# A later wait in the down product and an early Gelu table load in a fused decoder kernel

## Chip, cores and metric

The kernel runs on one core of a Trainium2 chip. The metric is the device time of one execution in microseconds (us), lower is better. The kernel before takes 1753.62 us, the median of three runs (1751.96 to 1753.97).

## What is computed

Eight sequences of 512 rows with 512 features go through one decoder layer, all in f32 unless said otherwise:

```python
x = layernorm(x + retention(x) + conv5(x))             # per-feature decay scan, then a 512x512 product
x = layernorm(x + mlstm_attention(q=x, k=ctx, v=ctx))  # 8 heads, gates from q, k, v
h = gelu([x, stats(x)] @ r1_w.T + r1_b)                # router, 6 statistics per row
probs = softmax(h @ r2_w.T)                            # 32 experts, each row picks two
# each expert takes its 160 best rows (capacity int(1.25 * 4096 / 32))
up = xe @ w_up.T; hact = silu(up[:, :1024]) * up[:, 1024:]
ye = hact @ w_down.T                                   # 512 outputs, weighted, added to the rows
# 16 adapters, one for every two experts: the same form with 128 hidden units
x = layernorm(x + experts + adapters)
```

## The kernel before

The work has three parts, one after the other. Every engine has its own program, and the order of work on each engine is written out by hand; engines wait for each other on counting semaphores.

**The pipeline over the sequences** (`run_pipeline`, L127) runs ten steps, n = 0 to 9. In step n the retention and the first norm of sequence n (flag `a`, true for n up to 7), the attention of sequence n - 1 (flag `s`, n from 1 to 8) and the last norm and router of sequence n - 2 (flag `r`, n from 2 to 9) are interleaved. ScalarE's order is in its `step` (L1054): the gates of sequence n (`gates_0`, `gates_1`, L955 to L969, which end with an Exp and a Ln), the copy of the router's statistics (`router_stats`, L1035), then `gates_3` and `gates_4` (L971 to L981, three Copies; the first waits for VectorE's running maximum, L1340), then the two Gelus of the router (`router_2`, L1042, which wait for TensorE's products L718 and L723), then `gates_5` (a Copy and two Exps, L1002 to L1004) and so on. Exp, Ln and Gelu need different function tables; the compiler puts an ACT_TABLE_LOAD straight before the ACTIVATE that needs another table, behind that instruction's waits written in the kernel. TensorE's router logits (L730) wait for the second Gelu, and its products for the attention state (L642) come after them. VectorE's work on the states (L1263) waits for L642.

**The selection** (L805 to L840 on TensorE) finds the rows of each expert.

**The experts**, 32 of them (`run_experts`, L133: two written out, 28 in a loop that handles two per turn, two written out). TensorE's order for one expert (`expert`, L888) is:

- `up` nine times (L853 to L870): chunk j of the hidden units, 128 of the gate and 128 of the values; j = 8 is the adapter's. Each f32 matmul counts as two in the trace, so this is 16 times 9 = 144 matmuls of 160 columns per expert on line L869. ScalarE makes the Silu of each chunk (L1144), VectorE multiplies (L1748, for the adapter L1750) and writes `hact[:, j]`. The steps of VectorE are named `mul0` to `mul8`.
- `rows_in` (L843 to L851): five transposes of the next expert's gathered rows (not in the last expert).
- `down` (L872 to L886): nine chunks again, 18 matmuls of 512 columns on L881 for the first 128 rows (k = 0), then 72 small ones on L884 for the other 32 rows (k = 1). At its head it waits for the weights, for `mul8`, and for the product before to have been read.

SyncE's queue loads the weights of expert e + 2 as soon as expert e has freed the buffers; GpSimd gathers rows and scatters results with indirect DMAs. Behind the last expert there is a tail: a last scatter, a gather of the rows that it touched, their norm and their store, while the other rows were normalised and stored beside the last two experts.

Of the kernel before, what the change touches and what calls it, by code (L numbers as in the profile page):

```python
# [21 lines left out]
ACT = mybir.ActivationFunctionType  # L22
# [3 lines left out]
NB, T, D = 8, 512, 512  # L26
# [3 lines left out]
TAPS, PAD = 5, 2  # L30
# [5 lines left out]
J = INTER // P  # L36
# [108 lines left out]
def decoder_kernel(nc, xT_d, kT_d, v_d, decay_d, WT_d, b_d, cw_d, cb_d, wi_d, wf_d, ib_d, fb_d, ln_d,  # L145
# [5 lines left out]
    with ctx:  # L151
# [5 lines left out]
        def steps(name, names, lead=3):  # L157
            p = Steps(sem(name), names, lead)
            every[name.split("_")[-1]].append(p)
            return p  # L160
# [36 lines left out]
        room = Room(arena, ROOM)  # L197
        WT = room.take(C, D)
        wgq = room.take(C, 32)
        wgk = room.take(C, 32)  # L200
# [10 lines left out]
        r1s = room.take(RH)  # L211
# [7 lines left out]
        xT = room.take(C, T + 2 * PAD)  # L219
# [14 lines left out]
        wgv = hg[:, 0, 0:C * 32].rearrange("p (c g) -> p c g", c=C)  # L234
        stT = gpart
        zeros = room.take(2 * D)
# [6 lines left out]
        Fr = [room.take(INT, dt=BF16) for _ in range(2)]  # L243
        Ff = g_rel.rearrange("p a t -> p (a t)")
        Fm = room.take(INT, dt=BF16)
        gm = room.take(T)
        bfs = [room.take(T, dt=BF16) for _ in range(2)]
# [22 lines left out]
        zeros = zeros[:, 0:D]  # L270
# [6 lines left out]
        oh0 = room.take(TB, NE)  # L277
        oh1 = room.take(TB, NE)
        wsum = room.take(TB)


        Wb = bank[0:2]
# [150 lines left out]
        up_v = steps("up_vector", [f"mul{j}" for j in range(J + 1)], 2)  # L433
# [106 lines left out]
        def _(pe):  # L540
# [285 lines left out]
            for i in range(2 * NT // LG):  # L826
                pe.wait_ge(*li_v.at(f"oh{i}", b0))
                k, lh = i * LG // NT, Lh[i % 3]
# [43 lines left out]
            def down(e):  # L872
                pe.wait_ge(ld_wd[e.slot], e.landed())
                pe.wait_ge(ld_ad[e.slot], e.landed())
                pe.wait_ge(*up_v.at(f"mul{J}", e))
                for k in range(2):
                    pe.wait_ge(*yr_v.at(f"y{k}", e - 1))
                    for j in range(J + 1):
                        w = wd[e.slot][:, j, :] if j < J else ad[e.slot]
                        if k == 0:  # L880
                            m = pe.matmul(Yb[0][:, :], hact[:, j, 0:P], w, start=(j == 0), stop=(j == J))  # L881
                        else:
                            for c in range(C):
                                m = pe.matmul(Yb[1][CAP2 * c:CAP2 * (c + 1), 0:P], hact[:, j, P:CAP],  # L884
                                              w[:, c * P:(c + 1) * P], start=(j == 0), stop=(j == J))
                    m.then_inc(yr_t(f"y{k}"), 1)  # L886
# [13 lines left out]
        def _(act):  # L900
# [5 lines left out]
            def inputs(b, c):  # L906

                if c == 0:
                    act.wait_ge(ld_x, b.line(16, 16))
                    act.wait_ge(*re_t.at(f"w{TB - 1}", b - 2))  # L910
                act.activation(ST[b.slot][:, c, :], xc[:, c, :], ACT.Identity, scale=a_one[:, c:c + 1])\
                    .then_inc(re_a(f"u{c}"), 1)
                act.activation(cv[b.slot][:, c, :], xc[:, c, :], ACT.Identity, scale=cw[:, c, PAD:PAD + 1],
                               bias=cb[:, c:c + 1]).then_inc(re_a(f"cv{c}"), 1)

            def raw_rows(b, tb):
                if tb == 0:
                    act.wait_ge(*ro_t.at("h1", b - 3))
                act.wait_ge(*re_t.at(f"w{tb}", b))
                act.activation(raw[:, tb, :], Wb[tb % 2][:, :], ACT.Copy).then_inc(n1_a(f"raw{tb}"), 1)  # L920

            def norm1_out(b):
                act.wait_ge(*n1_p.at("shift", b))
                act.wait_ge(*l2_v.at("sum", b - 2))
                for tb in range(TB):
                    act.activation(x1[b.slot][:, tb, :], raw[:, tb, :], ACT.Identity, scale=rs1[:, tb:tb + 1],
                                   bias=nb1[:, tb:tb + 1]).then_inc(n1_a(f"out{tb}"), 1)

            def norm3_out(b):
                act.wait_ge(*l2_p.at("shift3", b))  # L930
                act.wait_ge(*ro_v.at("stats", b - 1))
                for tb in range(TB):
                    act.activation(x2[b.slot][:, tb, :], x2[b.slot][:, tb, :], ACT.Identity, scale=rs3[:, tb:tb + 1],
                                   bias=nb3[:, tb:tb + 1], accum_out=rsum[:, tb:tb + 1]).then_inc(n3_a(f"out{tb}"), 1)

            def squares(b):
                act.wait_ge(*n3_a.at(f"out{TB - 1}", b))
                act.wait_ge(*ro_p.at("l2", b - 1))
                act.wait_ge(*ro_t.at("lg", b - 1))
                act.wait_ge(*ro_v.at("stats", b - 1))  # L940
                act.wait_ge(st_dum, 64)
                for tb in range(TB):
                    m = act.activation(sqr[tb], x2[b.slot][:, tb, :], ACT.Square,
                                       accum_out=rsq[:, tb:tb + 1])
                m.then_inc(n3_a("sq"), 1)
# [60 lines left out]
            def decays(b, h):  # L1006

                act.wait_ge(*bc_t.at(f"bc{h}", b))
                if h >= 4:
                    act.wait_ge(*pv_t.at(f"pv{h // 2 - 2}", b))  # L1010
                else:
                    act.wait_ge(*pv_t.at(f"pv{h // 2 + 2}", b - 1))
                if h == 0:
                    act.wait_ge(*ga_a.at("gcol", b))
                d = Dm[h // 2 % 2][:, h % 2 * T:(h % 2 + 1) * T]
                for tb in range(TB):
                    m = act.activation(d[:, tb * P:(tb + 1) * P], Bb[:, tb * P:(tb + 1) * P], ACT.Exp,  # L1017
                                       bias=gcol[b.slot][:, tb, h:h + 1])
                m.then_inc(at_a(f"exp{h}"), 1)
# [15 lines left out]
            def router_stats(b):  # L1035
                act.wait_ge(*ro_t.at("st", b))
                act.activation(stT[0:NSTAT], Tb[0:NSTAT, :], ACT.Copy).then_inc(ro_a("st"), 1)
# [6 lines left out]
            def router_3(b):  # L1044
# [2 lines left out]
                act.activation(lg, Wb[0][:, 0:TB * NE].rearrange("p (a e) -> p a e", a=TB), ACT.Copy)\  # L1047
                    .then_inc(ro_a("lg"), 1)

            def router_4(b):  # L1050
                act.wait_ge(*ro_v.at("lsub", b))
                act.activation(pr, pr, ACT.Exp).then_inc(ro_a("exp"), 1)

            def step(n, a, s, r, x1, x2):  # L1054

                if s:
                    decays(n - 1, 2)
                if x1:
                    inputs(n + 1, 0)
                if a:  # L1060
                    raw_rows(n, 0)
                if s:
                    decays(n - 1, 3)
                if x1:
                    inputs(n + 1, 1)
                if a:
                    raw_rows(n, 1)
                if x1:
                    inputs(n + 1, 2)
                if a:  # L1070
                    raw_rows(n, 2)
                if x1:
                    inputs(n + 1, 3)
                if s:
                    decays(n - 1, 4)
                if r:
                    norm3_out(n - 2)
                if a:
                    raw_rows(n, 3)
                if s:  # L1080
                    decays(n - 1, 5)
                if r and s:
                    squares(n - 2)
                if a:
                    norm1_out(n)
                    queries(n, (0, 1))
                if s:
                    decays(n - 1, 6)
                if a:
                    queries(n, (2, 3))  # L1090
                if r:
                    router_1(n - 2, a)
                if r and not s:
                    squares(n - 2)
                if s:
                    decays(n - 1, 7)
                if a:
                    gates_0(n)
                    gates_1(n)
                if r:  # L1100
                    router_stats(n - 2)
                if a:
                    gates_3(n)
                    gates_4(n)
                if r:
                    router_2(n - 2, 0)
                    router_2(n - 2, 1)
                if a:
                    gates_5(n)
                    gates_f(n)  # L1110
                    decays(n, 0)
                    gates_g(n)
                if r:
                    router_3(n - 2)
                if a:
                    decays(n, 1)
                    first_state(n)
                if r:
                    router_4(n - 2)
# [50 lines left out]
        def _(dve):  # L1170
            start(dve, "vector")

            for t in (xT[:, :, 0:PAD], xT[:, :, PAD + T:], wgq, wgk, wgv, gm, Fr[0], Fr[1], stT, r1s, bfs[0], bfs[1], zeros):
                dve.memset(t, 0.0)
            for t in va:
                dve.memset(t[:, :, NH * VW:], 0.0)
# [880 lines left out]
```

## Time and profile before

| what | value |
|---|---|
| median of three runs | 1753.62 us |
| profiled execution | 1756.21 us |
| its span, first to last instruction | 1754.4 us |
| TensorE matmul busy | 1504.7 us, 86% |
| VectorE busy | 758.7 us, 43% |
| ScalarE busy | 486.9 us, 28% |
| mean granted TensorE clock | 0.926 |

The profile comes from one execution; it lies 2.59 us above the median and 1.81 us of it lie outside the span. In the tables PE is TensorE's matmul side, PEld its weight loads, DVE VectorE, ACT ScalarE, POOL GpSimd, SP SyncE. A granted clock of 1.0 is 2.4 GHz, 0.5 is 1.2 GHz. The pipeline fills about the first 640 us, the selection runs to about 750 us, the experts to 1735 us.

### The profile page before, as it was taken

The numbers are of one execution on the slowest core, as the hardware profiler recorded it, in microseconds if no ns is written. First come the engines' busy times: TensorE is split into PE (matmuls) and PEld (weight loads), VectorE is DVE, ScalarE is ACT, GpSimd is POOL, SyncE is SP. The second block draws the span as 40 slices with busy tenths as digits, with TensorE's granted clock in tenths as the row PEclk, the third lists the DMA queues.
The fourth block names the chain that finished last, engine by engine and source line by source line (L and its number), as shares of the span: only waits on it lengthen the run. The fifth ranks groups of instructions, "written<-read, shape, count | busy, mean of one in ns | idle before, by whom it ended". The sixth has DMA issues, their size and how long they took to land.

```text
span 1754.4 us, 28619 instructions
## 1 busy us (share of the span) xinstructions
PE 1504.7 (86%) x11038; PEld 1158.6 (66%) x11076; DVE 758.7 (43%) x1783; ACT 486.9 (28%) x1165; POOL 309.4 (18%) x399
## 2 busy tenths in 40 slices
PE   3589999899897540389999999999999999999995
PEld 2256656556555420278787888878788887878884
DVE  7458999999978569811111111111111111111143
ACT  3446666676664220011111110111111011111123
POOL 3101121111111200011121212112121211212125
PEclk9698998998997765589999999999999999999998
DMA  5203123133211054046776767676776767677696
GB/s 156 72 1 115 48 79 104 48 90 95 75 49 49 1 202 169 0 156 214 285 246 259 264 222 282 214 283 240 264 264 226 278 215 278 239 271 257 230 344 209
DMA packets 92191, 311.02 MB, mean 177 GB/s; under 512 B 42455, under 2 KB 46557, under 8 KB 82781
## 3 DMA queue, kind: packets, MB, share of 16 engines
q1 hardware_dynamic: 78876, 287.87, 44.8%
q0 software_dynamic: 13248, 22.29, 5.6%
q8 instruction: 39, 0.64, 0.1%
q14 instruction: 28, 0.22, 0.0%
HBM read 273.18 MB, written 36.96 MB: 177 GB/s over the span
## 4 chain that ended last, share of the span: by engine, by line
PE 71%; DVE 18%; issue 6%; ACT 3%; DMA 1%; POOL 1%; SPq 0%; DVEq 0%; POOLq 0%; ACTq 0%
PE bank L869 36%; PE banks L881 15%; PE bank L582 5%; PE banks L884 4%; DVE arena L1212 3%; DVE arena L1587 2%; PE banks L672 2%; PE bank L718 1%; PE bank L584 1%; DVE arena L1202 1%; PE banks L683 1%; PE banks L656 1%; DVE arena L1378 1%; PE bank L642 1%; DVE arena L1233 1%
## 5 line engine op out<-in xcount | busy, mean ns | idle before, releaser
L869 PE MATMUL bank<-arena 128*128 128x160 f32 x4608 | 636.0, 300 | 0.7 <-issue 0.7
L869 PEld LDWEIGHTS bank<-arena 128*128 128x128 f32 x4608 | 628.3, 191 | 7.3 <-issue 7.3
L1144 ACT ACTIVATE arena<-bank 128x160 f32<-128x160 f32 x288 | 87.4, 303 | 835.2 <-PE bank L869 835.2
L1748 DVE TENSOR_TENSOR arena<-arena,bank 128x160 f32<-128x160 f32 x256 | 82.3, 322 | 459.4 <-ACT arena L1144 408.8
L881 PE MATMUL banks<-arena 128*128 128x512 f32 x576 | 255.6, 598 | 8.9 <-DVE arena L1750 8.9
L1914 POOL DMA_INDIRECT acc_rows<-arena,keep x64 | 102.8, 1606 | 651.9 <-DVE arena L1693 634.1
L881 PEld LDWEIGHTS banks<-arena 128*128 128x128 f32 x576 | 106.9, 190 | 138.6 <-issue 132.5
L1691 DVE TENSOR_SCALAR arena<-banks,keep 128x512 f32<-128x512 f32 x32 | 24.0, 750 | 318.8 <-PE banks L884 316.6
L582 PE MATMUL bank<-arena 128*128 128x512 f32 x256 | 121.7, 620 | 30.8 <-DVE arena L1212 30.8
L582 PEld LDWEIGHTS bank<-arena 128*128 128x128 f32 x256 | 49.8, 200 | 85.1 <-issue 77.1
L1212 DVE SCALAR_TENSOR_TENSOR arena<-arena 128x512 f32<-128x512 f32 x128 | 96.1, 750 | 3.4
L1017 ACT ACTIVATE arena<-bank,arena 128x128 f32<-128x128 f32 x256 | 72.5, 370 | 43.1 <-PE bank L557 43.1
L884 PEld LDWEIGHTS banks<-arena 128*32 128x32 f32 x2304 | 60.9, 110 | 24.3 <-issue 24.3
L672 PE MATMUL banks<-arena 128*128 128x96 f32 x512 | 71.6, 300 | 2.3 <-DVE arena L1293 2.3
L672 PEld LDWEIGHTS banks<-arena 128*128 128x128 f32 x512 | 68.7, 214 | 7.2 <-issue 7.2
L1902 POOL DMA_INDIRECT arena<-x_rows,keep x64 | 64.2, 1003 | 36.4 <-POOL keep L1894 26.6
L884 PE MATMUL banks<-arena 128*32 128x128 f32 x2304 | 69.5, 274 | 0.0
L1894 POOL COPY keep<-keep 128x2 int32 (+1 forms) x64 | 29.3, 458 | 204.9 <-DVE keep L1682 119.3
L718 PE MATMUL bank<-arena 128*128 128x512 f32 x128 | 60.7, 618 | 0.7 <-ACT arena L1031 0.7
L814 PE MATMUL bank<-arena 128*128 128x1 f16 x30 | 5.6, 185 | 59.2 <-DVE arena L1587 59.2
L1130 ACT ACTIVATE arena<-banks 128x512 f32<-128x512 f32 x32 | 19.1, 597 | 118.7 <-PE banks L850 114.9
L718 PEld LDWEIGHTS bank<-arena 128*128 128x128 f32 x128 | 23.9, 197 | 30.9 <-issue 29.5
(252 smaller groups left out, 1632.9 us busy)
## 6 DMA issues: line engine op xcount, KB each, us to landing
arena<-in_wup SPq DMA_DIRECT2D x32, 4096.0 KB, 12.5
arena<-in_wdn SPq DMA_DIRECT2D x32, 2048.0 KB
arena<-in_aup SPq DMA_DIRECT2D x32, 512.0 KB, 11.7
arena<-in_xT SPq DMA_DIRECT2D x8, 1024.0 KB, 5.3
arena<-in_kT SPq DMA_DIRECT2D x8, 1024.0 KB, 7.2
arena<-in_v SPq DMA_DIRECT2D x32, 256.0 KB, 7.8
x_rows<-arena SPq DMA_DIRECT2D x8, 1024.0 KB, 4.4
acc_rows<-arena SPq DMA_DIRECT2D x8, 1024.0 KB, 6.7
```

Of the source, the lines that this page charges most:

```text
L582: pe.matmul(w[:, :], ST[b.slot][:, c, rows], WT[:, c, :], start=(c == 0), stop=False)
L672: pe.matmul(Pp[:, r * T + tb * PVN:r * T + (tb + 1) * PVN], Dm[j % 2][:, r * T + tb * P:r * T + (tb + 1) * P], va[b.slot][:, tb, h * VW:h ...
L718: pe.matmul(Wb[k][:, :], r1x[:, c, k * P:(k + 1) * P], x2T[:, c, :], start=(c == 0), stop=False)
L869: m = pe.matmul(u[:, g * CAP:(g + 1) * CAP], w, xeT[:, c, :], start=(c == 0), stop=(c == C - 1))
L881: m = pe.matmul(Yb[0][:, :], hact[:, j, 0:P], w, start=(j == 0), stop=(j == J))
L884: m = pe.matmul(Yb[1][CAP2 * c:CAP2 * (c + 1), 0:P], hact[:, j, P:CAP], w[:, c * P:(c + 1) * P], start=(j == 0), stop=(j == J))
L1017: m = act.activation(d[:, tb * P:(tb + 1) * P], Bb[:, tb * P:(tb + 1) * P], ACT.Exp, bias=gcol[b.slot][:, tb, h:h + 1])
L1144: act.activation(sg[k], Ub[k][:, 0:CAP], ACT.Silu).then_inc(up_a(f"silu{j}"), 1)
L1212: dve.scalar_tensor_tensor(row, xT[:, c, k:k + T], cw[:, c, k:k + 1], row, ALU.mult, ALU.add).then_inc(re_v(f"tap{i}_{c}"), 1)
L1748: dve.tensor_tensor(hact[:, j, :], sg[k], u, ALU.mult).then_inc(up_v(f"mul{j}"), 1)
L1902: pool.indirect_dma_start(out=xg[e.slot][:, cols], out_offset=None, in_=rows, in_offset=bass.IndirectOffsetOnAxis(ap=idx_g[e.slot][:, k:k ...
L1914: pool.indirect_dma_start(out=rows, out_offset=bass.IndirectOffsetOnAxis(ap=idx_s[e.slot][:, k:k + 1], axis=0), in_=yy[e.slot][:, cols], i ...
```

## The change

```diff
+        tab = room.take(2)[0:1, 0:1]
...
             def down(e):
                 pe.wait_ge(ld_wd[e.slot], e.landed())
                 pe.wait_ge(ld_ad[e.slot], e.landed())
-                pe.wait_ge(*up_v.at(f"mul{J}", e))
+                pe.wait_ge(*up_v.at(f"mul{J - 1}", e))
                 for k in range(2):
                     pe.wait_ge(*yr_v.at(f"y{k}", e - 1))
                     for j in range(J + 1):
+                        if k == 0 and j == J:
+                            pe.wait_ge(*up_v.at(f"mul{J}", e))
                         w = wd[e.slot][:, j, :] if j < J else ad[e.slot]
...
+            def table(f):
+                act.activation(tab, tab, f)
+
...
                 if r:
                     router_stats(n - 2)
+                    table(ACT.Gelu)
                 if a:
                     gates_3(n)
                     gates_4(n)
...
-            for t in (xT[:, :, 0:PAD], xT[:, :, PAD + T:], wgq, wgk, wgv, gm, ...
+            for t in (xT[:, :, 0:PAD], xT[:, :, PAD + T:], wgq, wgk, wgv, tab, gm, ...
                 dve.memset(t, 0.0)
```

TensorE now enters `down` when `mul7` is there and waits for `mul8` only ahead of the ninth chunk of the first 128 rows. ScalarE gets one more ACTIVATE, a Gelu of one element in place, in each of the eight steps with `r`, between the copy of the router's statistics and `gates_3`. VectorE gets one more memset at its start.

## Rows read from the trace of the kernel before

**Rows 1.** The page: the chain that ended last, by line, share of the span

```profile
PE bank L869 36%; PE banks L881 15%; PE bank L582 5%; PE banks L884 4%; DVE arena L1212 3%; DVE arena L1587 2%; PE banks L672 2%; PE bank L718 1%; PE bank L584 1%; DVE arena L1202 1%; PE banks L683 1%; PE banks L656 1%; DVE arena L1378 1%; PE bank L642 1%; DVE arena L1233 1%
```

**Rows 2.** The chain in order of time, first and third expert: start us, us, what

```profile
751.90 21.38 PE bank L869 x144
...
815.05 19.77 PE bank L869 x144
...
835.64 7.99 PE banks L881 x18
...
845.73 19.77 PE bank L869 x144
```

**Rows 3.** Waits of TensorE by line: us in total, times, longest

```profile
PE banks L881 <- DVE arena L1750: 8.9, 32, 1.0
...
PE bank L730 <- ACT arena L1042: 5.9, 6, 1.8
```

**Rows 4.** Timeline, weight loads into down, four kinds of expert: start, length, idle before

```profile
926.46 0.60 PEld L850 LDWEIGHTS banks<-keep,arena 128*128 128x128 f32 x5
927.50 0.30 PEld L881 LDWEIGHTS banks<-arena 128*128 128x128 f32 x2 [0.44 <-DVE arena L1750]
...
958.17 0.30 PEld L881 LDWEIGHTS banks<-arena 128*128 128x128 f32 x2 [0.51 <-issue]
...
1693.54 0.30 PEld L881 LDWEIGHTS banks<-arena 128*128 128x128 f32 x2 [0.61 <-issue]
...
1724.31 0.30 PEld L881 LDWEIGHTS banks<-arena 128*128 128x128 f32 x2 [1.16 <-issue]
```

**Rows 5.** Timeline of TensorE's matmuls in the same expert as the first of rows 4

```profile
926.59 0.71 PE L850 MATMUL banks<-keep,arena 128*128 128x128 f32 x5
```

**Rows 6.** Timeline of VectorE in that expert: mul7, then mul8

```profile
924.95 0.32 DVE L1748 TENSOR_TENSOR arena<-arena,bank 128x160 f32<-128x160 f32 x1 [1.85 <-ACT arena L1144]
927.13 0.32 DVE L1750 SCALAR_TENSOR_TENSOR arena<-arena,bank 128x160 f32<-128x160 f32 x1 [1.85 <-ACT arena L1144]
```

**Rows 7.** Timeline of weight loads at the change from L881 to L884

```profile
934.48 0.19 PEld L881 LDWEIGHTS banks<-arena 128*128 128x128 f32 x1 [0.24 <-issue]
935.42 0.68 PEld L884 LDWEIGHTS banks<-arena 128*32 128x32 f32 x25 [0.76 <-issue]
```

**Rows 8.** Waits of TensorE's weight loads by line: us in total, times, longest

```profile
PEld bank L869 <- issue: 7.3, 32, 1.1
```

**Rows 9.** Stretches: busy of each engine, granted clock, DMA share, GB/s

```profile
755.00:1738.00 983.00, 970.52 (x7633) 810.10 (x7632) 149.87 (x427) 133.73 (x382) 190.53 (x220) 1.00 0.71 254
...
1660.00:1670.00 10.00, 9.80 (x37) 5.67 (x37) 0.64 (x2) 1.25 (x4) 0.00 (x0) 1.00 0.93 367
```

**Rows 10.** Timeline of SyncE's stores and of GpSimd in the tail

```profile
1701.33 29.83 SPq L534 DMA_DIRECT2D out<-arena  x8
...
1742.37 1.01 POOL L1960 DMA_INDIRECT out<-arena  x1 [0.30 <-issue]
```

**Rows 11.** Timeline of ScalarE in steps n = 3 and n = 7

```profile
262.68 0.63 ACT L976 ACTIVATE arena<-arena 8x512 bf16<-8x512 f32 x1 [4.17 <-DVE arena L1340]
...
528.19 0.63 ACT L976 ACTIVATE arena<-arena 8x512 bf16<-8x512 f32 x1 [2.63 <-DVE arena L1340]
```

**Rows 12.** Timeline of VectorE in steps n = 3 and n = 5, idle time ahead of L1263

```profile
279.47 0.43 DVE L1263 SCALAR_TENSOR_TENSOR arena<-arena,bank 128x260 f32<-128x260 f32 x1 [0.79 <-PE bank L642]
...
412.13 0.43 DVE L1263 SCALAR_TENSOR_TENSOR arena<-arena,bank 128x260 f32<-128x260 f32 x1 [0.58 <-PE bank L642]
```

**Rows 13.** Timeline of step n = 9 around the Gelus

```profile
629.06 1.88 PE L723 MATMUL bank<-arena 128*128 128x512 f32 x4
...
630.16 1.28 ACT L1042 ACT_TABLE_LOAD   x1 [3.76 <-PE bank L723]
631.46 1.26 ACT L1042 ACTIVATE arena<-bank,arena 128x512 f32<-128x512 f32 x2
...
632.78 1.41 PE L730 MATMUL bank<-arena 128*128 128x32 f32 x11 [1.83 <-ACT arena L1042]
```

More of the change, by code:

```diff
@@ L1171, in _ @@
             start(dve, "vector")
-            for t in (xT[:, :, 0:PAD], xT[:, :, PAD + T:], wgq, wgk, wgv, gm, Fr[0], Fr[1], stT, r1s, bfs[0], bfs[1], zeros):
+            for t in (xT[:, :, 0:PAD], xT[:, :, PAD + T:], wgq, wgk, wgv, tab, gm, Fr[0], Fr[1], stT, r1s, bfs[0], bfs[1], zeros):
                 dve.memset(t, 0.0)
```

## Prediction

> **What bounds the kernel now.** I read the page's chain first: the lines of the expert loop (L869, L881, L884) make up 55% of the span [rows 1], so the question for the first edit is what lies between them. The chain in order of time shows an expert as 19.77 us of L869, a hop over ScalarE and VectorE (L1750, which is `mul8`), 7.99 us of L881, which starts 0.82 us behind the end of L869, and L884; from one expert to the next it is 30.68 us [rows 2]. TensorE is never short of anything else there: in the stretch of the experts it is busy 970.5 of 983 us at the full clock, 2.4 GHz [rows 9]. Then the waits: L881 waits for L1750 in all 32 experts, 8.9 us together [rows 3]. That is only what the matmul side shows as idle; the weight loads, which run ahead of the matmuls, show more [rows 4]. For the second edit I looked at ScalarE in each of the eight steps with a router, and at who waits behind the Gelu: L730, six times, 5.9 us [rows 3]. Who waits is not yet who loses, since VectorE is mostly the busiest engine in the pipeline, so I went on to the idle time of VectorE behind it [rows 12].
>
> **The later wait, in the experts.** In a loop expert the five transposes of L850 follow each other at (0.71 - 0.27) / 4 = 0.11 us, 0.27 being the length of one [rows 5]. Their last weight load lasts 0.14 us and ends at 926.46 + 0.60 = 927.06, so it began at 926.92 [rows 4]. Without a wait the first weight load of L881 would begin one pitch later, at 927.03. It begins at 927.50: 0.47 us late, the idle 0.44 and the 0.03 by which a load is longer than the pitch. All of `down` hangs on it, so the whole 0.47 us is on the path; the page's 0.28 us per expert (8.9 / 32) understates it because a matmul's tail covers part of the hole. The other kinds come out in the same way from their idle time [rows 4]: the second expert of a loop turn 0.51 + 0.03 = 0.54 us, the first two and the one before the last 0.61 + 0.03 = 0.64 us, and the last expert, which has no transposes to fill the time, 1.16 + 0.05 = 1.21 us (a load of 0.19 at a pitch of 19.47 / 143 = 0.136).
>
> Is the new wait at the head of `down` free? `mul7` is written from 924.95 to 925.27, 1.76 us ahead of 927.03 [rows 6]: yes. Is the ninth chunk's? `mul8` is written by 927.45 [rows 6], while the ninth chunk is reached 16 matmuls of 0.43 us behind the first, at 933.9: yes, with 6.4 us to spare. What a wait that is already met costs in a stream of matmuls is shown by L869: eight such waits per expert stand inside its stream, and the only idle time of its weight loads is 7.3 us in 32 pieces, one per expert and therefore at its head [rows 8]. So it costs nothing at best; the other bound is below, among the rivals. The sum of the first edit:
>
> 14 x 0.47 + 14 x 0.54 + 3 x 0.64 + 1.21 = 6.58 + 7.56 + 1.92 + 1.21 = 17.3 us.
>
> What is late next? ScalarE and VectorE keep their distance to `up`, which is unchanged. The DMA queues must move the same bytes in 1.8% less time per expert: 254 GB/s become about 259, and one stretch of 10 us reached 367 [rows 9], so I cost that at nothing. In the last expert `down` moves forward by 1.2 us against the normalising of the other rows; their last store is issued at 1701.33 + 29.83 = 1731.2 and the store that needs all of them at 1742.4 [rows 10], 11 us later, so that cover is wide enough.
>
> **The early table, in the pipeline.** It adds a table load and an ACTIVATE of one element ahead of `gates_3`, and takes the table load ahead of the Gelu away; the Exps behind the Gelu load theirs as before, so the number of loads stays. The load takes 1.28 us [rows 13], the small ACTIVATE less than the 0.63 us of one of 512 elements on 8 partitions [rows 11]: at most 1.91 us together. ScalarE's wait there is 4.17 us in n = 3 (and in n = 2, 4, 5 and 6 the same) and 2.63 us in n = 7 [rows 11]; in n = 8 and 9 it is the wait for the hidden units, 3.76 us [rows 13]. The addition is covered everywhere, by 0.72 us at least. The Copies of `gates_3` and `gates_4` behind it need no table of their own (a Copy follows the Gelu now without a load, L1002), so nothing is loaded again.
>
> The Trainium skill, page ScalarE: Activation LUTs, section What ACT_TABLE_LOAD costs, prices a switch at about 2.66 us, of which 1.38 are a drain. By that price the addition would overrun the 2.63 us of n = 7, by 0.03 us and the length of the small ACTIVATE, and n = 9 would gain 1.38 us more than below. The trace does not show the drain: the ACTIVATE starts 1.30 us after the load's start [rows 13].
>
> What it gives back: in n = 9 nothing else is under way. The first Gelu could start when the first product is there, at 630.16 instead of 631.46; the second must wait for the second, 629.06 + 1.88 = 630.94, and ends about 0.74 us later, at 631.7, where it now ends at 632.72 [rows 13]. L730 gains 1.0 us. In n = 8 and n = 7 the Gelus are done before TensorE comes to L730 (no wait there in the trace): nothing. In n = 2 to 6 L730 waits for the Gelu, but VectorE is then busy without a break except in n = 3 and n = 5, where VectorE stands idle ahead of L1263 for 0.79 and 0.58 us [rows 12]. I take these two, since L642 moves with L730. Together 1.0 + 0.79 + 0.58 = 2.4 us. Bounds: zero, if VectorE's later work takes it all back, and the full load in every step, 8 x 1.28 = 10.3 us.
>
> The memset on one element lies ahead of VectorE's first wait for the input and of the loads of constants: 0 to 0.07 us, taken as nothing.
>
> **The sum.** 17.3 + 2.4 = 19.7 us. The profiled execution of 1756.2 us becomes 1736.5; it lies 2.6 us above the median, and from the median 1753.62 the same sum gives 1733.9 us. About 0.2%, 3.5 us, is what a measurement of this kernel can tell from no change. Its own range is 1731 to 1738: the pitch behind the transposes could be 0.03 us longer (0.8 us over 31), the table's part 0 to 3.7 us, and the first expert began while the clock was still low, which may fall otherwise when everything ahead of it moves (1.6 us, its 21.38 us of L869 against the later 19.77 [rows 2]).
>
> **The rivals.**
> - *Only the idle matmul time comes back.* The stream would close no further than the waits view says: 8.9 + 2.4 = 11.3 us, 1742.3 us. For it: the matmul side is what bounds. Against it: weight loads pace L850 and L881, and there the hole is larger.
> - *The table changes nothing.* Either the load is put elsewhere or VectorE takes the gain back: 1753.62 - 17.3 = 1736.3 us. For it: VectorE's near-unbroken work in n = 2 to 6.
> - *Every moved load pays in full:* 17.3 + 10.3 = 27.6 us, 1726.0 us. Against it: in four steps the trace shows no one late behind the Gelu but engines that wait anyway.
> - *The ninth-chunk wait breaks the stream (the slower side).* The first weight load of L884 also carries a wait, and it starts after 0.76 us of idle time, where the loads of L881 have 0.24 [rows 7]. If a wait inside `down` cost that whole 0.76 us at the ninth chunk, 32 x 0.76 = 24.3 us, the result were 1733.9 + 24.3 = 1758.2 us. It decides from 19.7 / 32 = 0.62 us per expert. If only the excess of 0.52 us were the wait's, 16.6 us would be lost, 1750.5 us. Against it: the eight waits inside L869 are free, and the hole at L884 comes with a change of the tile's shape, 128x128 to 128x32.
>
> **How the numbers follow.** Forecast 0.62; only idle matmul time 0.12; table nothing 0.14; every load in full 0.05; broken stream 0.04 at the full price (slower) and 0.03 at the part (counted within 0.2%). The likeliest case gives 1733.9. The range 1730 to 1742.5 takes in the forecast and the first two rivals, and leaves out 0.12. Faster 0.93, same 0.03, slower 0.04.
>
> **What would show it.** Right: L881 no longer waits for L1750; the weight load of L881 follows the last of L850 without idle time; the distance from expert to expert falls from 30.68 us to about 30.13 us and is the same in both kinds of loop expert; the table load of the Gelu stands behind L1037 in all eight steps, L730 waits in none of n = 2 to 6 for long, and in n = 9 starts about 1.0 us earlier behind L723. Wrong: idle time of weight loads ahead of the 17th of L881, a new wait for DMA at L869 or L850, an unchanged time at the end of the pipeline, or table loads that have become more than before.

## The result and the profile after

The changed kernel takes 1736.05 us (median of four runs, 1735.57 to 1740.62) against 1752.92 us before (four runs). The ratio is 0.9895 with a 95% interval from 0.9878 to 0.9913: some 18.4 us less, 1.05% (the two medians alone lie 16.9 us apart, and the interval spans 15.3 to 21.4 us). The forecast was 1733.9 us, with 19.7 us less. The profiled execution took 1735.57 us, its span 1733.8 us, 20.6 us less than the span of before.

From the page of the profile after, first the busy time of the engines, then the chain by line (the added lines shift the numbers: `down` is L884 and L887 now, `up` L870, the transposes L851, the logits L731):

```profile
PE 1487.3 (86%) x11038; PEld 1147.6 (66%) x11076; DVE 757.7 (44%) x1784; ACT 488.9 (28%) x1173; POOL 309.9 (18%) x399
...
PE bank L870 37%; PE banks L884 14%; PE bank L583 5%; PE banks L887 4%; DVE arena L1219 3%; DVE arena L1594 2%; PE banks L673 2%; DVE arena L1209 2%; PE bank L719 1%; PE bank L585 1%; PE banks L851 1%; PE banks L657 1%; DVE arena L1385 1%; 
```

The chain in order of time, a loop expert (start us, us, what), against [rows 2]:

```profile
809.97 19.76 PE bank L870 x144
829.73 0.55 PE banks L851 x5
830.27 7.73 PE banks L884 x18
838.00 2.10 PE banks L887 x72
840.11 19.76 PE bank L870 x144
```

ScalarE and VectorE have left the chain: between `up` and `down` stand only the five transposes, 0.55 us, and from expert to expert it is 30.14 us, where it was 30.60 us in one kind of loop expert and 30.68 in the other. The timeline of the weight loads in one loop expert, and its last row in the last expert, against [rows 4]:

```profile
919.84 0.60 PEld L851 LDWEIGHTS banks<-keep,arena 128*128 128x128 f32 x5
...
920.41 0.30 PEld L884 LDWEIGHTS banks<-arena 128*128 128x128 f32 x2
...
1703.30 0.33 PEld L884 LDWEIGHTS banks<-arena 128*128 128x128 f32 x2
```

There is no idle time in brackets: the first load of `down` starts at 920.41, 0.57 us behind the first transpose's, where it was 1.04 us before. The second load ends at 920.71 and the next starts 0.24 us later, the pace of the stream. In the last expert, which had 1.16 us of idle time, the load at 1703.30 has none either. The wait table of the weight loads:

```profile
PEld banks L884 <- issue: 122.4, 512, 0.2
PEld banks L887 <- issue: 24.3, 32, 0.8
PEld bank L870 <- issue: 7.3, 32, 1.1
```

The 7.3 and 24.3 us are those of before; no wait for VectorE is left at L884. 512 pauses are 16 per expert, the pace of the stream again, and none of them is longer than 0.2 us, so nothing stands ahead of the ninth chunk.

The pipeline: ScalarE in n = 7, where the covering wait was shortest, against [rows 11]:

```profile
524.55 1.28 ACT L1054 ACT_TABLE_LOAD   x1
525.85 0.20 ACT L1054 ACTIVATE arena<-arena 1x1 f32<-1x1 f32 x1
527.16 0.63 ACT L979 ACTIVATE arena<-arena 8x512 bf16<-8x512 f32 x1 [1.11 <-DVE arena L1347]
...
530.42 1.27 ACT L1045 ACTIVATE arena<-bank,arena 128x512 f32<-128x512 f32 x2
```

The load and the ACTIVATE of one element take 1.50 us together and leave 1.11 us of the wait; the Gelus start without a load. In n = 9, against [rows 13]:

```profile
625.87 1.88 PE L724 MATMUL bank<-arena 128*128 128x512 f32 x4
...
626.99 0.69 ACT L1045 ACTIVATE arena<-bank,arena 128x512 f32<-128x512 f32 x1 [2.26 <-PE bank L724]
627.84 0.69 ACT L1045 ACTIVATE arena<-bank,arena 128x512 f32<-128x512 f32 x1 [0.17 <-PE bank L724]
...
628.58 1.64 PE L731 MATMUL bank<-arena 128*128 128x32 f32 x13 [0.84 <-ACT arena L1045]
```

The logits (L731) start 2.71 us after the router's last products for the hidden units (L724), where it was 3.72 us: 1.01 us gained.

**Where the span's 20.6 us come from.** The chain's rows of the second expert's `up` and of the end of the last `down` in both traces: 784.28 and 1734.99 before, 779.84 and 1714.01 after. So 16.54 us were gained from the second expert on, where the forecast's terms for these 31 experts make 17.3 - 0.64 = 16.6. Ahead of that, 4.44 us: the first expert's `up` starts 4.27 us earlier (751.90 and 747.63), where the forecast had 2.4 us for the table. That difference was the open question. The two together are 20.98 us; the tail behind the last `down` gave 0.4 us back (its first transfer, of the touched rows, took 3.65 us for 3.36 before; in all traces it is 3.34 to 3.71 us with `down` as before and 3.51 to 3.86 us with the later wait).

### The profile page after: what moved, and what is told of

Its sections match the earlier page's. It is cut to its first block, busy times and chain, and to the rows that moved or that the text cites. A ratio compares the mean times of both kernels' runs of the same rounds, so it can differ in the third digit from the quotient of the medians.

```text
span 1733.8 us, 28656 instructions
## 1 busy us (share of the span) xinstructions
PE 1487.3 (86%) x11038; PEld 1147.6 (66%) x11076; DVE 757.7 (44%) x1784; ACT 488.9 (28%) x1173; POOL 309.9 (18%) x399
## 4 chain that ended last, share of the span: by engine, by line
PE 71%; DVE 19%; issue 5%; ACT 3%; DMA 1%; POOL 1%; SPq 0%; DVEq 0%; POOLq 0%; ACTq 0%
PE bank L870 37%; PE banks L884 14%; PE bank L583 5%; PE banks L887 4%; DVE arena L1219 3%; DVE arena L1594 2%; PE banks L673 2%; DVE arena L1209 2%; PE bank L719 1%; PE bank L585 1%; PE banks L851 1%; PE banks L657 1%; DVE arena L1385 1%; PE banks L684 1%; DVE arena L1240 1%
## 5 line engine op out<-in xcount | busy, mean ns | idle before, releaser
L870 PE MATMUL bank<-arena 128*128 128x160 f32 x4608 | 636.5, 300 | 0.7 <-issue 0.7
L870 PEld LDWEIGHTS bank<-arena 128*128 128x128 f32 x4608 | 628.8, 190 | 7.3 <-issue 7.3
L884 PE MATMUL banks<-arena 128*128 128x512 f32 x576 | 252.5, 592 | 0.0
L884 PEld LDWEIGHTS banks<-arena 128*128 128x128 f32 x576 | 107.0, 190 | 122.4 <-issue 122.4
L887 PEld LDWEIGHTS banks<-arena 128*32 128x32 f32 x2304 | 60.9, 110 | 24.3 <-issue 24.3
L887 PE MATMUL banks<-arena 128*32 128x128 f32 x2304 | 69.5, 274 | 0.0
L673 PEld LDWEIGHTS banks<-arena 128*128 128x128 f32 x512 | 64.6, 203 | 7.2 <-issue 7.2
L673 PE MATMUL banks<-arena 128*128 128x96 f32 x512 | 67.1, 288 | 2.3 <-DVE arena L1300 2.3
## 6 DMA issues: line engine op xcount, KB each, us to landing
arena<-in_aup SPq DMA_DIRECT2D x32, 512.0 KB, 11.6
```

Of the source, the lines that this page charges most:

```text
L673: pe.matmul(Pp[:, r * T + tb * PVN:r * T + (tb + 1) * PVN], Dm[j % 2][:, r * T + tb * P:r * T + (tb + 1) * P], va[b.slot][:, tb, h * VW:h ...
L870: m = pe.matmul(u[:, g * CAP:(g + 1) * CAP], w, xeT[:, c, :], start=(c == 0), stop=(c == C - 1))
```

## The experiments

All kernels were timed against the kernel before on the same chip. The parts first.

**The kernel before, against itself.**

> The kernel before, unchanged, against itself. Every theory: a ratio of 1 within 0.15%. Its profile is a second look at the kernel before: if the 3.3 us between the first profiled execution (1756.2) and the timed median (1752.9) come from the granted clock, this trace has the same 30.60 and 30.68 us per loop expert, and a different pattern of half-clock stretches ahead of 750 us, with the start of the first expert moved by up to 3 us.

Measured: 1756.78 us median of 12 runs (1751.97 to 1760.22) against 1753.83 us (23 runs, 1751.94 to 1760.78); ratio 1.0009, interval 0.9996 to 1.0021. The ratio holds. What matters is the spread: the same program varies over 8 us, and two medians of it differ by 3 us. In its profile the experts are as before, and the first expert starts within 1 us of the first trace (752.81 and 751.90), so this one profile does not show where the spread lies. Three kernels told below leave the pipeline as it was and change only `down`. Their first experts start at 756.59 us (the later wait alone), 747.98 us (the wait at each chunk) and 749.17 us (at the second chunk): with one and the same pipeline, 8.6 us lie between the first and the last. From there to the end of the span the three differ by 0.2 us. So in the traces the spread lies wholly ahead of the experts.

**The later wait alone.**

```diff
-                pe.wait_ge(*up_v.at(f"mul{J}", e))
+                pe.wait_ge(*up_v.at(f"mul{J - 1}", e))
...
+                        if k == 0 and j == J:
+                            pe.wait_ge(*up_v.at(f"mul{J}", e))
```

> The later wait alone, no table. Theory 1 (the whole hole in the weight loads comes back): 17.3 us less, ratio 0.990, loop experts 30.13 us apart, the pipeline as before. Theory 2 (only the matmul side's idle 8.9 us comes back and the pipeline gave the rest): 8.9 us less, ratio 0.995.

Measured: 1740.75 us (1736.84 to 1743.96), ratio 0.9916, interval 0.9898 to 0.9934, some 14.7 us (11.6 to 17.9). The trace decides between the theories more sharply than the times. Its chain:

```profile
788.30 19.76 PE bank L869 x144
...
818.43 19.76 PE bank L869 x144
838.19 0.55 PE banks L850 x5
838.74 7.73 PE banks L883 x18
...
1712.06 7.74 PE banks L883 x18
```

The experts are 30.13 us apart. From the second `up` to the start of the last `down` it is 923.76 us here and 1724.34 - 784.28 = 940.06 us before, 16.3 us less, and the last `down` itself is shorter by 0.2 (7.74 for 7.96). Theory 2, by which only 8.9 us would come back, has fallen. With the first expert, from its `up` to the end of the span, it is 985.5 us for 1002.5 before, 17.0 us less. But the first expert starts at 756.59, 4.7 us later than before, although nothing ahead of it was changed: the pipeline of this one execution was slower by more than the whole table was forecast to give, and the timed gain has the same uncertainty in it.

**The early table alone.**

```diff
...
+            def table(f):
+                act.activation(tab, tab, f)
...
                     router_stats(n - 2)
+                    table(ACT.Gelu)
```

> The early table alone, down as before. Theory 1: 2.4 us less (0 to 3.7), 1.0 of it in step n = 9, the rest in n = 3 and n = 5, experts 30.60 and 30.68 us apart. Theory 2: 8 us or more less, all ahead of the experts. Theory 3 (what the change gained ahead of the experts beyond 2.4 us was the clock's pattern of one execution): less than 2.4 us in the timed runs, with half-clock stretches that differ from both traces.

Measured: 1751.99 us (1750.92 to 1753.94, 11 runs), ratio 0.9986, interval 0.9976 to 0.9995: 2.4 us less (0.9 to 4.2); the medians are 1.8 us apart. The waits of this kernel: L882 (`down`) waits as before, and of the six waits of the logits one is left, in n = 9:

```profile
PE banks L882 <- DVE arena L1755: 8.9, 32, 1.0
PE bank L731 <- ACT arena L1043: 0.8, 1, 0.8
```

Its trace gives 4.6 us ahead of the experts, the timed runs 2.4 us. Theory 2 is out. Theory 3 asked for less than 2.4 us in the timed runs, which they do not show; what they do show is that one trace overstates the table.

**The change a second and a third time.**

> The change as it stands, a second time on the same chip as the parts. If the parts add up: the sum of the two gains within 1.5 us, about 17.3 + 2.4 = 19.7 us or ratio 0.989. If the table's part depends on the granted clock: the sum of the parts missed by more than that, and executions that spread by several us.

Measured: 1735.06 us (1734.75 to 1738.02, 5 runs), ratio 0.9892, interval 0.9878 to 0.9907: 18.9 us. The parts' ratios add up to 14.7 + 2.4 = 17.1 us. That is 1.8 us short of it, a little more than I allowed, and within the interval of the later wait alone, which is 6 us wide.

> The change as it stands once more, as the measure for the two kernels that follow on the same chip. Ratio 0.989 within 0.15%.

Measured: 1736.15 us (1735.31 to 1738.01), ratio 0.9893, interval 0.9877 to 0.9908, as expected.

**Where the table counts.** Two kernels with `down` as before.

The first has the table in the last two steps alone:

```diff
-                    table(ACT.Gelu)
+                    if not a:
+                        table(ACT.Gelu)
```

The second in the first six alone:

```diff
-                    table(ACT.Gelu)
+                    if a:
+                        table(ACT.Gelu)
```

> The early table only in the two steps without gates, n = 8 and 9; down as before. Forecast's account: L730 of n = 9 comes 1.0 us earlier against its step, nothing in n = 8; 1.0 us less. If the 1.85 us that step n = 8 gained with the whole change belong to its own table load, they are here too: 2.9 us less. If they come from the granted clock, which follows what TensorE did in n = 7, they are not: the half-clock stretches behind 545 us stay in two parts, as in the kernel before.

> The early table only in n = 2 to 7; down as before. Forecast's account: 1.4 us less, from n = 3 and 5. If the clock is what the table changes: the two half-clock stretches of 10 us in n = 3 and n = 5 are gone or shorter, the stretch behind 543 us is one piece and n = 8 is 1.8 us shorter although it has no early table itself, some 3 us less in the trace; and the timed executions spread over about 3 us, as with the table everywhere, and not over the 8 us of the kernel before.

Measured: both 0.9998, with intervals of 0.9989 to 1.0008 and 0.9988 to 1.0009; medians 1755.11 and 1754.49 against 1754.63 us. The times cannot tell either from no change; a gain of 1.0 us, and for the second one of 1.4 us, lies inside both intervals. The spread that I expected of the second, 3 us, was 6.7 us (1751.74 to 1758.43), so the clock theory was wrong in that: the table in the first six steps does not make the executions alike. Nor was the whole table's 2.4 us found in the two parts. The traces say more, step by step. In n = 9 the first has its 1.0 us:

```profile
630.82 1.88 PE L724 MATMUL bank<-arena 128*128 128x512 f32 x4
633.54 1.97 PE L731 MATMUL bank<-arena 128*128 128x32 f32 x16 [0.84 <-ACT arena L1043]
```

that is 2.72 us from product to logits, as with the whole change. The length of n = 8 is read between the chain's rows of VectorE's first statistics in n = 8 and in n = 9. In the kernel before, run against itself:

```profile
547.24 2.39 DVE arena L1300 x4
598.44 2.48 DVE arena L1300 x4
```

With the table in the last two steps:

```profile
550.16 2.39 DVE arena L1306 x4
599.36 2.48 DVE arena L1306 x4
```

The wait at each chunk, a kernel told below, which has no early table at all:

```profile
544.79 2.39 DVE arena L1302 x4
593.65 2.48 DVE arena L1302 x4
```

Step n = 8 takes 51.20 us in the first, 49.20 us in the second and 48.86 us in the third; the same rows give 49.28 us with the table in the first six steps, so without one in n = 8, and 49.34 us in the changed kernel. It is 51.16 us with the later wait alone and 49.11 us with the wait at the second chunk, both without a table. So the 1.9 us that n = 8 gained between the two traces are not the table's own. The granted clock is what differs. In the kernel before TensorE was at 1.2 GHz in two pieces, the second of which lasted to about 28 us into the step and covered the attention's products; in the one with no table and the short step it was at 2.4 GHz from 566.7 us on, 22 us into the step. The kernel with the table in the last two steps was at 1.2 GHz without a break up to 22 us into the step, and at 2.4 GHz behind that: its step is a short one, so it is the stretch behind the 22 us that costs, and the expectation that this kernel would keep the two pieces was wrong. The windows of n = 8 in the kernel before, from its first profile (stretch, its length, busy of PE, PEld, DVE, ACT, POOL, granted clock, DMA share, GB/s):

```profile
563.90:574.20 10.30, 9.89 (x54) 8.58 (x55) 9.63 (x20) 4.04 (x15) 1.54 (x3) 0.50 0.55 206
```

And in the kernel with a wait at each chunk:

```profile
566.70:574.20 7.50, 5.28 (x46) 3.97 (x47) 6.71 (x20) 4.23 (x12) 3.02 (x7) 1.00 0.20 74
```

**What a met wait inside the stream costs.** This kernel and the next have no early table; the edits are against the kernel before.

```diff
-                pe.wait_ge(*up_v.at(f"mul{J}", e))
+                pe.wait_ge(*up_v.at("mul0", e))
...
+                        if k == 0 and j:
+                            pe.wait_ge(*up_v.at(f"mul{j}", e))
```

> The later wait taken further: down starts behind mul0 and waits for each of the nine units ahead of its own chunk, eight waits inside the stream instead of one, all met long before. If a met wait inside a stream of matmuls is free (the forecast): experts 30.13 us apart, as with the later wait alone. If it costs the 0.09 us by which the first product of L884 comes late, or more: 7 x 0.09 = 0.6 us more per expert, 30.8 us apart or worse. Starting behind mul0 brings nothing, since mul7 is there in time; at most the last expert gains 0.1 us.

Measured: 1735.13 us in its one run, which tells little beside runs that spread over several us; it is as fast as the whole change, without a table, because its first expert starts early, as said above. The chain tells more:

```profile
809.69 19.76 PE bank L869 x144
829.45 0.55 PE banks L850 x5
829.99 7.73 PE banks L883 x18
...
839.82 19.76 PE bank L869 x144
```

30.13 us apart and `down` at the same 7.73 us with eight waits inside the stream as with one. A met wait is free here. The slower rival, which priced the wait at up to 0.76 us, has fallen: the pause of 0.76 us ahead of the small products of k = 1 (in all 32 experts, in this kernel as in the changed one) is there whatever the waits are.

**How much cover the wait needs.**

```diff
-                pe.wait_ge(*up_v.at(f"mul{J}", e))
+                pe.wait_ge(*up_v.at(f"mul{J - 1}", e))
...
+                        if k == 0 and j == 1:
+                            pe.wait_ge(*up_v.at(f"mul{J}", e))
```

> The wait for the adapter's unit at the second chunk instead of the ninth. If all that matters is when mul8 is written (0.42 us behind the point at which down could start in a loop expert) and a chunk of the first 128 rows takes 0.86 us, then one chunk hides it: loop experts 30.13 us apart, as with the ninth chunk; the last expert, where mul8 comes 0.98 us behind that point, loses 0.1 to 0.4 us. If the wait has to be far from its product because TensorE's sequencer must see it met many instructions ahead: part of the 0.47 to 0.54 us per expert is lost again, 30.3 to 30.6 us apart.

Measured: 1736.33 us in its one run. In the loop `up` starts at 810.96 and at 841.09, 30.13 us apart: one chunk hides what eight do, but only just. The weight loads reach the second chunk at 831.53 us, and `mul8` was written at 831.41. Only in the last expert it shows, where no transposes stand between. The chain of the last expert:

```profile
1684.82 19.76 PE bank L869 x144
1704.58 7.90 PE banks L883 x18
```

And the weight loads there, in the timeline:

```profile
1705.33 0.30 PEld L883 LDWEIGHTS banks<-arena 128*128 128x128 f32 x2 [0.72 <-DVE arena L1752]
```

7.90 us for 7.72 us in the changed kernel's last expert: 0.18 us, at the lower end of the 0.1 to 0.4 expected. So what matters is when `mul8` is written against when its chunk is reached, and not how far the wait lies ahead in TensorE's program. The row shows one thing more. The idle 0.72 us are 0.48 us above the pace of 0.24, and yet `down` lost only 0.18 us. Inside `down` the loads pause for 0.24 us at each step in any case, and part of a late load goes unnoticed there. Behind the transposes, where the loads follow each other without a pause, the whole hole was lost.

**Two attempts at a better version.** The first hides the table of the router's Exp in the same manner in n = 8 and 9, the second also that of the gates' Ln in n = 0 to 7 (each small ACTIVATE reads a constant and writes a word of its own); the edit of the first, and what the second has beside it:

```diff
                     router_2(n - 2, 1)
+                    if not a:
+                        act.activation(tabe, ones[0:1], ACT.Exp)
```

```diff
                     gates_0(n)
+                    act.activation(tabl, ones[0:1], ACT.Ln)
                     gates_1(n)
```

> The whole change and, in the two steps without gates, one more ACTIVATE of one element behind the two Gelus, an Exp, so that the table for the router's Exp is loaded while TensorE makes the logits. If a load counts only where ScalarE's chain is alone: step n = 9 loses the 1.28 us that stand between the logits' copy and the Exp, n = 8 nothing (its load lies in a wait of 3.2 us for VectorE), 1.3 us less than the change as it stands, all at the end of the pipeline. If the clock gives it back: less than 0.5 us in the timed runs.

Measured: 1735.99 us (1735.74 to 1736.53), ratio 0.9891, interval 0.9875 to 0.9906, against 1736.15 us and 0.9893 for the change itself on the same chip: no difference that the times can tell. In the trace of n = 9:

```profile
629.09 1.28 ACT L1117 ACT_TABLE_LOAD   x1
...
631.13 0.28 ACT L1051 ACTIVATE arena<-bank 128x128 f32<-128x128 f32 x1 [0.55 <-PE bank L732]
632.09 0.31 ACT L1059 ACTIVATE arena<-arena 128x128 f32<-128x128 f32 x1 [0.68 <-DVE arena L1407]
```

Here the expectation was wrong by its own terms: between the copy of the logits and the Exp VectorE has 0.66 us of its own work, the subtraction of the maximum, which the load had covered. So 0.6 us were to be had, not 1.28. The first expert's `up` starts at 748.07 us, against 748.37 in the change's third profile and 747.63 and 747.61 in the first two, so the traces cannot tell what is left of the 0.6 us. Nothing that can be measured came of it.

> As before it and, in each step with gates, a Ln of one element ahead of the gates, in ScalarE's wait of about 2.1 us for the gates' sum. If the table that is loaded for it serves the Exp of the gates too: one load less between Exp and Ln, the log comes 1.28 us earlier in n = 0 to 7; on the path that is in n = 0 and n = 1, where VectorE waits for the log, not in n = 2 to 6, where it is busy. 1.3 to 2.6 us less than the kernel before it. If the Exp asks for another table: two more loads per step, 8 x 2.6 us of ScalarE's time, slower by 3 to 8 us.

Measured: 1741.92 us (1741.28 to 1744.38), ratio 0.9926, interval 0.9912 to 0.9939: 5.8 us slower than the change itself. The Exp does ask for another table. ScalarE in n = 7:

```profile
521.17 0.20 ACT L1107 ACTIVATE arena<-keep 1x1 f32<-1x1 f32 x1
...
523.91 1.28 ACT L972 ACT_TABLE_LOAD   x1
525.20 0.63 ACT L972 ACTIVATE arena<-arena 8x512 f32<-8x512 f32 x1
525.85 1.28 ACT L974 ACT_TABLE_LOAD   x1
```

A load ahead of the Exp (L972) and another ahead of the Ln (L974, as before), behind the one for the small Ln: 16 loads more in the execution. The load for the small Ln lies in ScalarE's wait for the gates' sum, which was 2.08 us in the changed kernel. The one at L972 lies ahead of the log, on the gates' path. Neither attempt is measurably better than the change as it stands.

## Why the prediction was right

**The later wait: right, term by term.** The forecast said 0.47 and 0.54 us per loop expert, 0.64 for the others, 1.21 us for the last. Both kinds of loop expert are now 30.13 to 30.14 us apart; from the second `up` to the end the trace gives 16.54 us for a sum of 16.6, and the later wait alone 16.3 + 0.2. From the start of the first expert to the end of the span it is 985.3 to 986.2 us in every trace with the later wait, and 1002.2 to 1003.1 us in every one without it. The step that carried it was to read the hole where the weight loads show it [rows 4] and not from the waits of the matmul side [rows 3]; the first rival, which took the 8.9 us, was wrong by half. The cost of nothing for the ninth chunk's wait came from L869's eight free waits [rows 8], and a kernel with eight such waits in `down` bears it out. No wait for DMA appeared at `up` or at the transposes, beyond the one ahead of the first expert that was there before, and the tail stayed covered as argued.

**The early table: right in n = 9, not shown in n = 3 and n = 5.** The sum had 0.79 + 0.58 + 1.0 us. In n = 9 it is 1.01 us. In n = 3 VectorE's idle time ahead of the states [rows 12] is gone: L1270, the line of L1263 before, starts at 278.70 instead of 279.47; in n = 5 it is gone, too. But the step of the prediction behind these two terms, that VectorE stands idle there because the logits wait for the Gelu, does not hold by itself. The kernel before, run against itself, has the same wait of the logits in n = 5, the full clock behind it, and no idle time of VectorE (the logits in the timeline, the window from there to L1263, and L1263 itself, with nothing in brackets):

```profile
403.14 1.97 PE L730 MATMUL bank<-arena 128*128 128x32 f32 x16 [0.82 <-ACT arena L1042]
```

```profile
403.10:413.20 10.10, 7.18 (x98) 6.28 (x100) 9.82 (x14) 6.42 (x18) 0.00 (x0) 1.00 0.01 2
```

```profile
413.19 0.42 DVE L1263 SCALAR_TENSOR_TENSOR arena<-arena,bank 128x260 f32<-128x260 f32 x1
```

In the trace of the prediction TensorE was at 1.2 GHz in parts of both stretches (a mean granted clock of 0.59 ahead of L1263 in n = 3, 0.60 in n = 5), and the idle time needs those slower products. That the logits' wait of 0.81 us has its part in it fits the sum, but no trace shows it: in the traces with the table the clock there is 1.00, so they cannot say what the earlier Gelu alone would have brought. From n = 2 to n = 6, between the rows of L1378 (L1385 after), it is 265.74 us before and 264.88 after, 0.86 us less for the 1.37 of the forecast. The other five traces without a table in these steps have 264.84 to 267.60 us, and the other five with it 264.91 to 265.03 us (the kernel with the small Ln left out). So the table comes with a steadier and mostly shorter pipeline there, of which the direct gain of the forecast is at best a part; the times cannot tell it from nothing. The changed kernel's trace also has a half-clock stretch at 345.6 to 349 us, at the start of n = 5, in which the trace of before has none: from n = 4 to n = 5 the same rows are 67.01 us apart for 65.99 before (windows of n = 3 and n = 5 in the changed kernel, granted clock in the column after the engines):

```profile
270.40:280.60 10.20, 6.31 (x81) 4.52 (x83) 9.87 (x15) 3.30 (x11) 0.00 (x0) 1.00 0.03 4
345.60:349.00 3.40, 3.40 (x5) 1.35 (x4) 3.19 (x10) 0.56 (x3) 0.00 (x0) 0.50 0.85 251
```

The term that was mis-sized is the table's 2.4 us, if one goes by the two profiled executions: 4.27 us, of which 1.9 are step n = 8, which is shorter in kernels without the table, too. By the timed runs it is 2.4 us with the table everywhere, and not told from nothing with the table in either part of the steps. That they give the forecast's number is in part luck, since only 1.0 us of it is shown where the forecast put it. The rival that the table changes nothing (1736.3 us) lies within the noise of the medians and nearer to the measured 1736.05 us than the forecast; against it speak the 1.01 us in n = 9, in every trace with the table there, and the interval of the table alone, which ends below 1, if only just.

**The measured time is 2.1 us above the forecast.** The same sum, taken from a profiled execution, was set on a median that had been 2.6 us below that execution. The medians of the kernel before in these comparisons went from 1752.9 to 1755.2 us, so the level is uncertain by about that, and the ratios, 0.9892 to 0.9895, say 18.4 to 19.0 us for a forecast of 19.7. In the profiled execution the first expert took back part of it: it ran at 1.2 GHz for some 4.1 us and before for 3.1, 21.83 us of L870 against 21.38. The earlier start is not the reason, since the kernel with a wait at each chunk starts it at 747.98 us and needs 21.20 us. The forecast had named this first expert as uncertain and priced it at up to 1.6 us; it cost 0.45 us. Why the executions of one program spread over 8 us ahead of the experts stays open beyond this: the half-clock stretches lie differently in every trace without an early table, and almost alike in the six traces with it in n = 2 to 7 (the kernel with the small Ln left out), but the timed runs with the table in the first six steps spread all the same.

The Trainium skill, page ScalarE: Activation LUTs, section What ACT_TABLE_LOAD costs, gave about 2.66 us for a switch, drain included. The trace does not agree: in n = 7 the load and the small ACTIVATE behind it end 1.50 us after the load's start, and the 2.63 us wait that the page's price would have overrun had 1.11 us left.

## What to carry to other kernels

Where one engine bounds a loop, let its stream start on the parts that are ready and put the wait for the last part at the place that needs it: one chunk hid a delay of 0.4 us, and eight waits inside the stream cost no more than one. Where the weight loads follow each other without a pause, read such a hole from their start to start, since the matmuls' own idle time showed only half of it; where the loads pause anyway, a hole costs less than they show (0.18 us of 0.48). A small ACTIVATE that loads a table early showed its gain only where nothing but the ScalarE chain was on the path, and it can force loads elsewhere, so count the loads in the trace after it. Idle time that stands behind a half-clock stretch in one trace should be looked for in a second trace of the same kernel before it is put into a sum. When single executions spread over 8 us, compare a gain between two marks behind the spread, here from the first expert on, where the later wait stood clear in every trace.

## What the runs showed of the hardware

- Ln and Exp, called one behind the other in this kernel, did not share the table that the Ln had loaded: a load stood ahead of each, 1.28 us apiece, also with a Ln just ahead. Both functions ran from different tables before the change, too, so this was there to be seen.
- The stretches at half clock moved with small changes of what came ahead. TensorE was busy 9.53 of 10.2 us at half clock in n = 3 of the kernel before against itself, and 6.31 us at the full clock in the changed kernel for the same products; between the rows of L1378 a step of 66.0 us lost 0.9 to 1.5 us by such a stretch, while VectorE was busy 9.22 of the 10.2 us, and n = 8 lost 1.9 us, where the chain goes through the attention's products. The window of n = 3 in the kernel before against itself:

```profile
271.30:281.50 10.20, 9.53 (x83) 8.41 (x85) 9.22 (x14) 4.38 (x13) 0.00 (x0) 0.50 0.08 11
```
